# Attention projections as three one-pass products in fills of 512 columns, and two token tiles per output-projection job

## The reference

```
q = rope(x Wq^T + bq)   k = rope(x Wk^T + bk)   v = x Wv^T + bv     16 heads of 16
attn = softmax(q k^T / 4)            per sequence and head, 1024 x 1024
x1   = layernorm(x + (attn v) Wo^T + bo)
out  = layernorm(x1 + (moe0(x1) + moe1(x1)) / 2)
moe  : logits = x1 router; top 2 of 32 experts by softmax score;
       y = sum over the two of score * (silu(x1 wg) * (x1 wu)) wd      hidden 128
```

## Time and profile before

| | before |
|---|---|
| median of 3 runs | 2279.51 us (2279.37 to 2288.64) |
| span of the profiled execution | 2348.8 us |
| PE busy | 2205.4 us (94%) |
| DVE busy | 1774.4 us (76%) |
| ACT busy | 1599.4 us (68%) |
| POOL busy | 1037.2 us (44%) |
| mean DMA traffic | 155 GB/s |
| attention, from the first score product of sequence 0 | 88 to about 1650 us |

### The profile page before, as it was taken

How to read it: one execution, slowest core, us unless ns; L and a number is a source line. 1 busy time by engine, 2 the same in 40 slices (tenths; PEclk the granted TensorE clock), 3 DMA queues, 4 the chain that set the end, 5 groups by cost and what they waited for, 6 DMA issues and landing times.

```text
span 2348.8 us, 46747 instructions
## 1 busy us (share of the span) xinstructions
PE 2205.4 (94%) x13885; PEld 1125.7 (48%) x13893; DVE 1774.4 (76%) x3301; ACT 1599.4 (68%) x3621; POOL 1037.2 (44%) x886
## 2 busy tenths in 40 slices
PE   8999999999999999999999999999888888999994
PEld 4433343433433343344344344333476666777773
DVE  6988888889898889889988888985247443346666
ACT  1488877786887878688687778868534333566674
POOL 3131240334436354343635534433556555555552
PEclk9999999999999999999999999998899999999997
DMA  6334442444543454454355444646655467799886
GB/s 178 91 87 90 122 95 53 132 109 116 160 117 95 140 155 114 118 144 134 85 161 150 103 123 141 185 125 191 190 164 167 135 182 226 226 330 298 285 272 204
DMA packets 179667, 363.70 MB, mean 155 GB/s; under 512 B 31009, under 2 KB 113185, under 8 KB 175329
## 3 DMA queue, kind: packets, MB, share of 16 engines
q1 hardware_dynamic: 150408, 282.67, 44.1%
q0 software_dynamic: 27552, 75.67, 8.9%
q10 hardware_dynamic: 1464, 2.38, 0.4%
HBM read 196.78 MB, written 136.03 MB: 142 GB/s over the span
## 4 chain that ended last, share of the span: by engine, by line
PE 78%; DVE 11%; issue 4%; ACT 2%; DMA 1%; another core or an unknown queue 1%; POOL 1%; SPq 1%; ACTq 0%; DVEq 0%; POOLq 0%
PE ps_a L990 24%; PE ps_o L1009 20%; PE ps_a L1797 7%; DVE maxima_sb L1242 7%; PE ps_b L908 5%; PE ps_b L1821 4%; PE ps_b L1797 3%; PE ps_b L980 3%; PE ps_b L918 3%; PE ps_a L1784 3%; PE ps_o L1821 2%; PE ps_b L1806 2%; ACT probs_sb L845 1%; PE ps_b L928 1%
## 5 line engine op out<-in xcount | busy, mean ns | idle before, releaser
L1242 DVE TENSOR_REDUCE maxima_sb<-ps_a 128x1 f32<-128x1024 f32 x1024 | 1233.8, 1220 | 184.1 <-PE ps_a L990 164.4
L845 ACT ACTIVATE probs_sb<-ps_b 128x512 f32<-128x512 f32 x2013 | 1087.2, 600 | 283.7 <-PE ps_b L980 244.3
L990 PE MATMUL ps_a<-k_stack_sb,q_stack_sb 48*128 48x512 f32 x2048 | 736.4, 444 | 25.6 <-DVE maxima_sb L1242 23.8
L980 PE MATMUL ps_b<-q_stack_sb,k_stack_sb 50*128 50x512 f32 x2013 | 745.3, 450 | 4.2 <-ACT probs_sb L845 2.6
L1009 PE MATMUL ps_o<-probs_sb,v_sb_sb 128*32 128x512 f32 (+1 forms) x5400 | 586.7, 507 | 0.7 <-ACT probs_sb L845 0.5
L990 PEld LDWEIGHTS ps_a<-k_stack_sb,q_stack_sb 48*128 48x128 f32 x2048 | 304.8, 185 | 552.5 <-issue 281.5
L1648 POOL DMA_INDIRECT y_dram<-y_rows_sb,spot_sb x318 | 313.5, 986 | 258.1 <-DVE y_rows_sb L2110 107.9
L174 POOL DMA_INDIRECT rows_dram<-stage_sb,listed_sb x208 | 202.6, 974 | 306.1 <-PE ps_o L1009 280.4
L980 PEld LDWEIGHTS ps_b<-q_stack_sb,k_stack_sb 50*128 50x128 f32 x2013 | 305.5, 186 | 47.5 <-ACT probs_sb L845 39.2
L1797 PE MATMUL ps_a<-w_gu_sb,x_cols_sb 128*128 x848 | 226.1, 390 | 4.5 <-ACT x_cols_sb L1704 2.8
L1009 PEld LDWEIGHTS ps_o<-probs_sb,v_sb_sb 128*32 128x32 f32 x5400 | 106.6, 108 | 236.1 <-issue 107.7
(11 more groups left out here) (249 smaller groups left out, 2369.2 us busy)
## 6 DMA issues: line engine op xcount, KB each, us to landing
x_rows_sb<-rows_dram SPq DMA_DIRECT2D x318, 129.5 KB
sums_rows_sb<-y_dram SPq DMA_DIRECT2D x40, 512.0 KB
parts_dram<-parts_q_sb SPq DMA_DIRECT2D x16, 1024.0 KB
parts_dram<-parts_k_sb SPq DMA_DIRECT2D x16, 1024.0 KB
q_stack_sb<-parts_dram SPq DMA_DIRECT2D x62, 256.0 KB
k_stack_sb<-parts_dram SPq DMA_DIRECT2D x62, 256.0 KB
swapped_sb<-feat_qk_sb SPq DMA_DIRECT2D x60, 256.0 KB
stage_sb<-x_dram SPq DMA_DIRECT2D x56, 256.0 KB
```

What stands on the lines that cost most here:

```text
L845: act.activation(probs[t % NPR][:, j, :], src[:, :], ACT.Exp, scale=float(DH) ** -0.5).then_inc(s_bdrain, 1)
L980: pe.matmul(out[:, :], k_stack[u % NSTK][lo:lo + XROWS, jj, kc * P:(kc + 1) * P].bitcast(F32R), q_stack[u % NSTK][lo:lo + XROWS, jj, qh * ...
L990: ins = pe.matmul(out[:, kh, :], q_stack[u % NSTK][lo:lo + ROWS, jj, qt * P:(qt + 1) * P].bitcast(F32R), k_stack[u % NSTK][lo:lo + ROWS, j ...
L1242: vec.tensor_reduce(maxima[u % 2][:, 1 - k, i:i + 1], src[:, :, :].rearrange("p a q -> p (a q)"), AX.X, ALU.max).then_inc(s_adrain, 1)
```

## The change

For sequences 1 to 7 x and the weights of Q, K and V are cut into an upper part, rounded to float32r, and the rest. A product is then three one-pass products (upper x upper, upper x lower, lower x upper: `PRODUCTS`) in place of one float32 product. Q and K are computed in halves of 512 tokens (8 jobs in place of 16 for a sequence), V two token tiles per job (4 in place of 8). POOL makes the parts of x (`x_split`, a CAST and a subtraction) for half of the tokens at a time, four times per sequence, since both halves are needed for c = 0 and again for c = 1; SP loads x by halves, four times. `w_split` makes the weights' parts once. Sequence 0 keeps its quarters in float32.

POOL also makes the upper part of rotated Q and K, by a CAST (`part`), in place of DVE's bit mask; the features live in the tiles of the parts. O takes two token tiles per job: 4 jobs at steps 22, 24, 26 and 28 in place of 8 at 22 to 29, `add_heads` 128x512 at once. In `chain_at` scale, T, L and top2 come earlier or later by some steps. `between` now carries its room over from step to step: what a step overdraws is a debt of the next.

```diff
-        for c, at in enumerate((start - 56, start - 33 if b else start - 21)):
-            for q in range(QUARTERS):
-                put(b_jobs, at + q, "Q", b, c, q)
-                put(b_jobs, at + QUARTERS + q, "K", b, c, q)
-        for i in range(KC):
-            put(b_jobs, start - 7 + i, "V", b, i)
+        if b == 0:
+            for c, at in enumerate((start - 56, start - 21)):
+                for q in range(QUARTERS):
+                    put(b_jobs, at + q, "Q", b, c, q)
+                    put(b_jobs, at + QUARTERS + q, "K", b, c, q)
+            for i in range(KC):
+                put(b_jobs, start - 7 + i, "V", b, i)
+        else:
+            for c in range(DC):
+                for h in range(2):
+                    at = start + PHASE_AT[2 * c + h]
+                    put(b_jobs, at, "Q", b, c, h)
+                    put(b_jobs, at + 2, "K", b, c, h)
+                    if c == 1:
+                        for i, v in enumerate(V_AT[h]):
+                            put(b_jobs, start + v, "V", b, 2 * h + i)
         if b == nb - 1:
             continue
         at = chain_at(nb, b)
-        for i in range(KC):
-            put(a_jobs, at["O"] + i, "O", b, i)
+        for i in range(KC // 2):
+            put(a_jobs, at["O"] + 2 * i, "O", b, i)
...
-        at = dict(O=22, norm=23, scale=39, T=48, L=50, x1=48, top2=57, exp=67, route=73, choose=74, marks=75, R=78, ranks=79,
-                  rank_sums=80, choices=86)
+        at = dict(O=22, norm=23, scale=40, T=44, L=46, x1=44, top2=50, exp=73, route=74, choose=75, marks=76, R=78, ranks=79,
+                  rank_sums=80, choices=85)
...
+PRODUCTS = ((0, 0), (0, 1), (1, 0))
...
-SPLIT_STEPS = 8
+SPLIT_STEPS = 10
+PHASES = 4
+PHASE_AT, V_AT = (-57, -48, -28, -15), ((-24, -22), (-6, -2))
+X_AT, X_SPLIT_AT = (-65.5, -54, -45, -21), (-61, -51, -37, -18)
...
-        k_step = lambda b, c: SPB * b + (-48, -16)[c]
-        pool_order = []
+        k_step = lambda b, c: SPB * b + ((-45, -12) if b else (-48, -16))[c]
+        x_no = lambda b, phase: PHASES * (b - 1) + phase
+        x_used = lambda b, phase: (b_no[("K", b, 0, phase)] if phase < 2 else b_no[("V", b, 2 * phase - 3)]) + 1
+        pool_order = [(1, "w_parts", ())]
+        for b in range(1, nb):
+            for phase in range(PHASES):
+                pool_order.append((max(SPB * b + X_SPLIT_AT[phase], 3), "x_parts", (b, phase)))
...
-        def lower(eng, b, c, which):
+        def part(eng, b, c, which):
 
             n = b * DC + c
-            eng.wait_ge(s_mask, 2 * n + which + 1)
-            if n:
-                eng.wait_ge(s_parts, 16 * 2 * n)
+            at = pool_no[("split", (b, c))] + 6 + 2 * which
+            if which == 0 and c == 1 and b >= 2:
+                eng.wait_ge(s_afill, a_no[("L", b - 2, KC // 2 - 1)] + 1)
+            eng.wait_ge(s_parts, 16 * 2 * n)
             if n == 1:
                 eng.wait_ge(s_stack[0], stack_full(0))
-            eng.tensor_tensor(parts[which][:, 1, :], feat[which][:, :], parts[which][:, 0, :],
-                              ALU.subtract).then_inc(s_pool, 1)
-
-        def upper(vec, b, c, which):
-            n = b * DC + c
-            vec.wait_ge(s_pool, pool_no[("split", (b, c))] + 3 * (which + 1))
-            if which == 0 and c == 1 and b >= 2:
-                vec.wait_ge(s_afill, a_no[("L", b - 2, KC // 2 - 1)] + 1)
-            if n:
-                vec.wait_ge(s_parts, 16 * 2 * n)
-            if n == 1:
-                vec.wait_ge(s_stack[0], stack_full(0))
-            vec.tensor_scalar(parts[which][:, 0, :].bitcast(I32), feat[which][:, :].bitcast(I32), TOP12, None,
-                              ALU.bitwise_and).then_inc(s_mask, 1)
+            eng.wait_ge(s_pool, at)
+            eng.tensor_copy(parts[which][:, 0, :].bitcast(F32R), feat[which]).then_inc(s_pool, 1)
+            eng.wait_ge(s_pool, at + 1)
+            eng.tensor_tensor(feat[which], feat[which], parts[which][:, 0, :], ALU.subtract).then_inc(s_pool, 1)
+
+        def x_split(eng, b, phase):
+
+            n = x_no(b, phase)
+            eng.wait_ge(s_xt, 16 * (n + 1))
+            eng.tensor_copy(x_parts[:, 0], x_in).then_inc(s_xupper, 1)
+            eng.wait_ge(s_xupper, n + 1)
+            eng.tensor_tensor(x_parts[:, 1], x_in, x_parts[:, 0].bitcast(F32), ALU.subtract).then_inc(s_xlower, 1)
+
+        def w_split(eng):
+
+            eng.wait_ge(s_bfill, max(b_no[("K", 0, 1, QUARTERS - 1)], b_no[("V", 0, KC - 1)]) + 1)
+            eng.tensor_copy(w_upper[:, :, :, :], w_qkv[:, :, :, :]).then_inc(s_wparts, 1)
+            eng.wait_ge(s_wparts, 1)
+            eng.tensor_tensor(w_lower[:, :, :, :], w_qkv[:, :, :, :], w_upper[:, :, :, :].bitcast(F32), ALU.subtract).then_inc(s_wparts, 1)
...
+            def next_x(b, phase):
+                h = phase % 2
+                if (b, phase) == (1, 0):
+                    sp.wait_ge(s_bfill, max(b_no[("K", 0, 1, QUARTERS - 1)], b_no[("V", 0, KC - 1)]) + 1)
+                elif phase == 0:
+                    sp.wait_ge(s_bfill, x_used(b - 1, PHASES - 1))
+                else:
+                    sp.wait_ge(s_bfill, x_used(b, phase - 1))
+                sp.dma_start(x_in, dram["x_t"][b, :, :, h * HALF:(h + 1) * HALF]).then_inc(s_xt, 16)
...
+            def features(which, b, c, h):
+                out = b_tile()
+                pe.wait_ge(s_wparts, 2)
+                pe.wait_ge(s_xlower, x_no(b, 2 * c + h) + 1)
+                for n, (dc, w, x) in enumerate((dc, w, x) for dc in range(DC) for w, x in PRODUCTS):
+                    ins = pe.matmul(out[:, :], (w_upper, w_lower)[w][:, which, dc, c * P:(c + 1) * P],
+                                    x_parts[:, x, dc, :], start=n == 0, stop=n == DC * len(PRODUCTS) - 1)
...
+            def values(b, i):
+                out = b_tile()
+                pe.wait_ge(s_xlower, x_no(b, 2 + i // 2) + 1)
+                for a in range(2):
+                    at = (2 * i + a) % (KC // 2) * P
+                    for n, (dc, w, x) in enumerate((dc, w, x) for dc in range(DC) for w, x in PRODUCTS):
+                        ins = pe.matmul(out[:, a * D:(a + 1) * D], x_parts[:, x, dc, at:at + P],
+                                        (w_upper, w_lower)[w][:, 2, dc, :], start=n == 0, stop=n == DC * len(PRODUCTS) - 1)
...
-                for c in range(DC):
-                    ins = pe.matmul(out[:, 0, 0:D], o_feat[b % 2][:, c, i * P:(i + 1) * P], w_o[:, c, :],
-                                    start=c == 0, stop=c == DC - 1)
+                for a in range(2):
+                    for c in range(DC):
+                        ins = pe.matmul(out[:, a, 0:D], o_feat[b % 2][:, c, (2 * i + a) * P:(2 * i + a + 1) * P], w_o[:, c, :],
+                                        start=c == 0, stop=c == DC - 1)
...
-                vec.tensor_tensor(y[:, i, :], src[:, 0, 0:D], y[:, i, :], ALU.add).then_inc(s_adrain, 1)
+                vec.tensor_tensor(y[:, 2 * i:2 * i + 2, :], src[:, :, 0:D], y[:, 2 * i:2 * i + 2, :], ALU.add).then_inc(s_adrain, 1)
...
-                    chores += [(end + 8, 1, recip(b)), (at["norm"], 2, norm(b)), (at["top2"], 3, top2(b)), (at["route"], 4, route(b)),
-                               (at["marks"], 4, marks(b)), (at["ranks"], 5, ranks(b)), (at["choices"], 6, ranks_of_choices(b))]
+                    chores += [(end + 8, 0, recip(b)), (at["norm"], 2, norm(b)), (at["top2"], 3, top2(b)), (at["route"], 0, route(b)),
+                               (at["marks"], 0, marks(b)), (at["ranks"], 0, ranks(b)), (at["choices"], 0, ranks_of_choices(b))]
...
+            room = [0]
 
             def between(t):
                 held = [name for name, *_ in b_jobs.get(t, []) + a_jobs.get(t, [])]
                 if t + LEAD >= n_steps:
-                    room = 1 << 30
+                    room[0] = 1 << 30
                 elif t >= SPB * (nb - 1):
-                    room = 4
+                    room[0] = min(room[0], 0) + 6
                 elif "O" in held:
-                    room = 5
+                    room[0] = min(room[0], 0) + 12
+                elif any(name in held for name in "QKV"):
+                    room[0] = min(room[0], 0) + 14
                 else:
-                    room = 7 if any(name in held for name in "QKV") else 0
+                    room[0] = min(room[0], 0) + (5 if "T" in held else 2)
                 while True:
-                    ready = [x for x in chores if x[0] <= t and (room > 0 or x[1] == 0)]
+                    ready = [x for x in chores if x[0] <= t and (room[0] > 0 or x[1] == 0)]
                     if not ready:
                         break
```

118 lines of the change are left out of this document (69 added, 49 removed).

## The result

| | before | changed |
|---|---|---|
| median | 2279.44 us (2278.08 to 2288.64, 4 runs) | 2329.66 us (2315.55 to 2344.61, 4 runs) |
| ratio | | 1.020 (1.0145 to 1.0262) |
| profiled execution, span | 2348.8 | 2323.6 |

The account below looks back on a forecast made before the run. TensorE (78% of the chain) bounds, VectorE and ScalarE close behind. Sequences 2 to 6: 8.6 - 1.5 - 1.8 - 3.8 - 1.0 - 0.9; all sequences and vanished stalls: 4.7 us less, 2275 us, range 2256 to 2297.

Parts of the forecast that it names:

- Jobs on TensorE: Fewer, longer one-pass jobs: steps of 3.83, 3.87 and 4.25 us, saving 8.6 us per sequence, 5.5 of it Q/K/V.
- Rival D: One-pass products on TensorE take 0.33 us, not 0.213: 50 us more, 2328 us; chance 0.04.
- POOL's cast: POOL's new CAST of 128x1024 for the parts of x: 1.2 us, bounds 0.9 and 2.85.
- A: Rival: the gain comes through, POOL's cast costs 0.9 us, clock holds, split_max slips past POOL; 2262 us, chance 0.22.
- B: Rival: POOL becomes the bound, its CAST taking 2.85 us; 2300 us, slower; chance 0.15.
- The wait at step 16: TensorE waits for POOL's second x split behind norm_o: 3.4 us per sequence, 6.3 in sequence 1 with the first split.
- The lock: VectorE's split_max stalls beside a busy POOL at steps 26 and 58: 1.0 us per sequence, bounds 0 to 2.4.
- rival C: VectorE instructions with two SBUF inputs, sixteen MAX_INDEX per sequence, are held up: 4 to 5 us each sequence, 2300; chance 0.06.
- The clock: After the step 16 wait TensorE may run at granted 0.50: 0.9 us per sequence, bounds 0 and 1.7.
- Chores: VectorE chores landing on quiet steps give back 1.5 us per sequence, bounds nothing and about 4.
- the sign that I had named: Prediction wrong if step 16 has no wait, or quiet steps grow by more than 0.2 us on the mean.
- ScalarE's 1.8: Copies of pv's result and scaling on ScalarE meet quiet steps: 1.8 us lost per sequence, bounds 0 and 4.8.

Follow-up runs that it names:

- e2: Changed kernel with exp, route, choose and marks one step earlier; ratio 1.022 (1.015 to 1.029) to the kernel before.
- e1: Changed kernel with row maxima handed over whole by one one-input reduction, replacing split_max's mask and subtraction; ratio 1.008 (1.0038 to 1.0126) to the kernel before.
- e13: e12 with split_max's original mask and two-input subtraction put back; ratio 1.0165 (1.011 to 1.022) to the kernel before.
- e12: e9 with the second feature half's Q and K jobs at steps 39, 41, 51, 53 and first V jobs at 35, 37; ratio 1.003 (0.999 to 1.007).
- e8: Kernel before with two useless VectorE reductions (or one) at steps 20 and 44 of sequences 1 to 6; with two, those sequences took 1241.9 us.
- e11: The changed kernel itself, measured again; ratio 1.021 (1.017 to 1.026) to the kernel before.
- e6: e5 with the V jobs of steps 40 and 42 moved to 30 and 32; ratio 1.016 (1.013 to 1.020) to the kernel before.
- e9: e5 with ScalarE scaling one token tile per step from step 37 and the three choices in step 20; ratio 1.0075 (1.004 to 1.011).
- e8_one: Kernel before with one useless VectorE reduction at steps 20 and 44 of sequences 1 to 6; those sequences took 1208.5 us.
- e5: e4 with the second pair of Q and K jobs at steps 18 and 20 in place of 16 and 18; ratio 1.0025 (0.999 to 1.006).
- e14: e12 with the first half's rotation, parts and stacks (SyncE turns, POOL place) two steps later; ratio 1.007 (1.004 to 1.0105).
- e15: e12 with the stack's DMA issued behind the previous unit's o_raw copies on SyncE's queue; 2266.51 us, ratio 0.9937 (0.9903 to 0.9972).
- e4: Changed kernel with maxima handed over whole, marks a step earlier and choices waiting for room; ratio 1.008 (1.004 to 1.011).

## Why the prediction was wrong, step by step

**Jobs on TensorE: right in kind, priced a little too cheap.** A K step of the changed kernel (the job begins at 722.21):

```profile
719.89 0.50 PE L1069 MATMUL ps_a<-k_stack_sb,q_stack_sb 48*128 48x512 f32 x1
...
723.78 0.49 PE L1069 MATMUL ps_a<-k_stack_sb,q_stack_sb 48*128 48x512 f32 x1
```

3.89 against my 3.83, V 3.94 against 3.87, O 4.24 against 4.25. 4.7 us per sequence for Q, K, V in place of 5.5. Rival D is out: its 2328 (by its own sum 2325) lies beside the measured 2329.66 by coincidence.

**POOL's cast: right.** 1.04 us, midway between the 0.9 of A and my 1.2. B is out.

**The wait at step 16: the mechanism right, the addition wrong.** (25.8 and 3.8 less 26.1 is 3.5, not 3.4.) In sequence 1, where no marks stand ahead, TensorE idled 5.0 there, and step 16 took 10.24, 6.3 over its kind, half clock included. In sequences 2 to 6 it held 1.3, until e2 removed the lock of the marks and it held 4.8. I added stalls that lie one behind the other on the same path; they overlap.

**The lock: the step that failed.** I priced 1.0 us per sequence, for split_max alone, and gave rival C, two-input instructions, a chance of 0.06 because of one row, the scan beside L470. That row was true and told of something else: it shows one scan, begun 0.9 us into a TENSOR_SCALAR of POOL. Beside POOL's TENSOR_TENSOR the same scan behaves otherwise; the scan of sequence 3 before, with POOL idle, then POOL and the scan in the changed kernel:

```profile
721.76 1.26 DVE L1159 TENSOR_TENSOR_SCAN incl_sb<-scan_bf_sb,totals_sb 128x512 f32<-128x512 bf16 x1
...
745.82 2.38 POOL L479 TENSOR_TENSOR x_parts_sb<-x_t_sb,x_parts_sb 128x1024 fp32r<-128x1024 f32 x1
...
746.95 2.33 DVE L1238 TENSOR_TENSOR_SCAN incl_sb<-scan_bf_sb,totals_sb 128x512 f32<-128x512 bf16 x1
```

2.33 where it takes 1.20 to 1.26 alone; in sequence 7, begun 0.5 us into POOL's L516, it took 1.67, so that even beside a TENSOR_SCALAR it isn't free. In the changed kernel, among the instructions of VectorE with two inputs from SBUF, the marks (up to 2.89 for 0.68), split_max's subtraction (up to 2.39 for 0.19), the choices' L1260 (up to 1.22 for 0.19) and the scan (up to 2.60), begun inside a POOL TENSOR_TENSOR, all end a fixed time behind its end: 0.55, 0.05, 0.05 and 1.08 us. The Trainium skill (SBUF — State Buffer, "Who interferes with whom") says that a VectorE instruction with two SBUF inputs contends with one of GpSimd that reads SBUF, and the trace agrees, but for MAX_INDEX (FIND_INDEX8 in the trace): 45 of them started inside a POOL TENSOR_TENSOR or CAST and took 0.18 as ever, so the place where rival C looked was the wrong one. The trace of the kernel before could have told it: 66 of its MAX_INDEX started inside a POOL TENSOR_TENSOR and took 0.18 to 0.19. Adding one input from PSUM (L1147) was never held either. The price: in the changed kernel's sequences 2 to 6 the steps behind split_max (27, 28, 59) held 4.0 more per sequence than in e1, where I had 1.0, and e13 against e12 gives 30 us, 4.3 per sequence; the marks, scan and choices come on top, each hidden in part by a later wait.

**The clock: right in kind, too cheap.** I took 0.9 per sequence. The changed kernel had ten stretches of 3.4 us at half clock in sequences 2 to 6, two per sequence, which cost 3.4 us together, and 27.3 us in sequence 0. The e8 runs show it apart from the stall. It is why the two profiled executions of the changed kernel (this one and e11) differ by 8.3 us in sequence 0; how much of the 29 us between its runs comes from there isn't shown.

**Chores: too cheap.** I took 1.5 for VectorE. (By the sign that I had named, quiet steps longer by over 0.2 on the mean, the prediction would have stood: they grew from 2.55 to 2.71, and step 16 had its wait.) Route's reduction at step 11 (1.3 over) and the three choices in one step (1.9 at 22, half clock included) were bursts of priority 0; I had counted their length, not that they stand together. ScalarE's 1.8 was close: 2.6 at steps 42 to 46, and e6 and e9 put most of it on the scaling.

**By sequence.** For sequence 0 I had -3.2 and it took +10.4; without the lock (e1) -3.4. For sequence 1 I had +1.6 and it took +4.1. For sequences 2 to 6, gains of before's stalls included, I had -0.3 each and they took +6.6: short by 6.9. For sequence 7 I had -1.5 and got -6.9, by luck: in the trace of the kernel before TensorE waits for ScalarE at 1587.2, near the end of that sequence, and then runs 17.1 us at half clock (1588.8 to 1605.8).

```profile
1587.17 0.49 PE L980 MATMUL ps_b<-q_stack_sb,k_stack_sb 50*128 50x512 f32 x1 [1.89 <-ACT probs_sb L845]
```

e8_one, which has the code of before in sequence 7 and no half clock there, takes 124.4 us from its first scores to the last score product, the kernel before 131.9 and the changed one 124.9. So the change gained some 1 us in sequence 7 at most (its trace has 3.4 us of half clock there), and against an execution of before without that stretch its loss inside attention would be some 50 us, not 42.8 (an estimate: 42.8 and 7.5).

**A wait behind each wait.** I closed each term with the place that it would show, and never asked what stands two or three steps behind in the chain job, swap, rotation, parts, stack. e2, e5, e9, e12 and e14 found one each time: the split, the choices with half clock, the drain on the parts' DMA, the copies of o_raw, K's parts behind stage_in. What remains open is how much of e15's 8 to 12 us per sequence over the kinds is still of that sort.

## What to carry to other kernels

When work moves onto POOL, list every VectorE instruction with two SBUF inputs, and every mask like L1169, that will run in the same steps, and price each at the rest of POOL's instruction, unless rows show that this pair of operations runs side by side; one row clears only the pair that it shows. A stall of TensorE costs itself and can cost a stretch at half clock: in e8 it followed seven of twelve stalls of 1.4 to 1.7 us, in the changed kernel eleven of twelve of 2.0 and more, and in e8 with one reduction none, where a stall cost its step 0.61 or less. And a kernel in which VectorE and ScalarE are busy for 2.34 and 2.40 us of a quiet step's 2.46 has waits standing behind waits: here a gain came only with e15, behind the edits of e4, e5, e9 and e12.

## What the runs showed of the hardware that was not expected

- VectorE and POOL hold each other both ways: L516 of POOL took 3.69 in four places and 3.17 in one, in place of 2.84 to 2.86, each time with a mark beside it.
- A one-input mask (L1169, 128x32) was held too, up to 2.20 for 0.17: the eleven that began inside a CAST or TENSOR_TENSOR of POOL all ended 0.03 to 0.08 behind its end. A TENSOR_REDUCE of the same tile (e1) took 0.18 beside them.
- Half clock behind the stalls of e8, 1.4 to 1.7 us, lasted 3.4 to 13.7 us, and after five of twelve didn't come. In the changed kernel's attention it began at or behind eleven of the twelve idle stretches of TensorE of 2.0 us and more, once for 27.3 us, and one of the eight between 1.3 and 1.8.
- The expert phase, whose code the change leaves alone, took some 670 us in some executions and some 740 in others, in versions of both kernels. No run here explains it.
